# An expert layer on one core: results read back from the last put with pairs, and gathers that skip unused list places

## The reference

```python
h2 = _rmsnorm(x, ffn_norm_w).reshape(Bx * Tx, Dx)
glogits = h2 @ gate_w + gate_b
topv, topi = jax.lax.top_k(glogits, TOPK)      # TOPK = 4 of E = 32
gw = jax.nn.softmax(topv, axis=-1)
combine = jnp.zeros((N, E), x.dtype).at[jnp.arange(N)[:, None], topi].add(gw)
def body(acc, we):
    wu, wd, ce = we
    ug = h2 @ wu
    u, g = (ug[:, :DFF], ug[:, DFF:])
    return (acc + ce[:, None] * (jax.nn.silu(g) * u @ wd), None)
y2, _ = jax.lax.scan(body, jnp.zeros_like(h2), (W_up, W_down, combine.T))
return x + y2.reshape(Bx, Tx, Dx)
```

## Time and profile before

| | |
|---|---|
| median of 3 runs | 1138.51 us (1137.43 to 1142.05) |
| the profiled execution | 1133.5 us |
| its span, first to last instruction | 1131.7 us |
| busy PE, DVE, POOL, ACT | 87%, 73%, 62%, 40% of the span |
| granted TensorE clock, mean | 0.918 |
| DMA | 239.22 MB, mean 211 GB/s |
| software queue (POOL's transfers) | 40.02 MB in 19552 packets |
| expert loop, first transpose to first final sum | 676.6 to 1098.4 us |

### The profile page before, as it was taken

How to read it: one execution, slowest core, us unless ns; L and a number is a source line. 1 busy time by engine, 2 the same in 40 slices (tenths; PEclk the granted TensorE clock), 3 DMA queues, 4 the chain that set the end, 5 groups by cost and what they waited for, 6 DMA issues and landing times.

```text
span 1131.7 us, 19754 instructions
## 1 busy us (share of the span) xinstructions
PE 984.0 (87%) x6270; PEld 795.6 (70%) x6270; DVE 829.8 (73%) x1750; ACT 456.6 (40%) x1120; POOL 700.9 (62%) x654
## 2 busy tenths in 40 slices
PE   3879699998999989989987419999999999999995
PEld 2557477676776776757766308888888888888884
DVE  3878589778787788877957526777777677777778
ACT  1123243342432423333344205555555555555541
POOL 1404435757747667576585856777777777777750
PEclk8779799889898898988999659999999999999997
DMA  6237976566566555574665467776776767766599
GB/s 188 69 87 237 326 255 187 157 198 179 176 181 207 161 167 190 179 217 136 186 204 194 154 231 261 266 257 246 255 245 212 250 228 250 257 212 209 133 336 372
DMA packets 110748, 239.22 MB, mean 211 GB/s; under 512 B 19170, under 2 KB 48247, under 8 KB 109914
## 3 DMA queue, kind: packets, MB, share of 16 engines
q1 hardware_dynamic: 84042, 192.03, 51.8%
q0 software_dynamic: 19552, 40.02, 11.1%
q10 hardware_dynamic: 7056, 5.91, 1.6%
HBM read 140.37 MB, written 90.05 MB: 204 GB/s over the span
## 4 chain that ended last, share of the span: by engine, by line
PE 38%; DVE 22%; POOL 18%; issue 14%; DMA 6%; ACT 1%; SPq 0%; DVEq 0%; POOLq 0%; ACTq 0%
POOL rows_in L685 7%; PE gbank L985 7%; PE gbank L852 6%; DVE ring L1354 6%; POOL pick_rows L692 4%; POOL lists L647 4%; PE scores L813 4%; DMA rows_in<-x_rows,token_row 4%; PE gbank L1005 3%; PE gbank L777 3%; PE gbank L748 2%; POOL ring L654 1%; DVE stat L1368 1%; PE gbank L767 1%; DVE prob L1390 1%
## 5 line engine op out<-in xcount | busy, mean ns | idle before, releaser
L985 PE MATMUL gbank<-ring,in_part 128*128 x954 | 262.8, 411 | 0.1
L654 POOL TENSOR_TENSOR ring<-ring 128x512 fp32r<-128x512 f32 x96 | 121.5, 1281 | 141.7 <-ACT ring L1151 141.1
L692 POOL DMA_INDIRECT pick_rows<-rows_out,pair_row x156 | 161.6, 1036 | 56.5 <-issue 46.9
L985 PEld LDWEIGHTS gbank<-ring,in_part 128*128 128x128 f32 x954 | 168.6, 190 | 28.7 <-issue 0.3
L685 POOL DMA_INDIRECT rows_in<-x_rows,token_row x156 | 151.7, 972 | 54.2 <-issue 34.3
L647 POOL DMA_INDIRECT lists<-entry,slot_i x128 | 136.1, 1063 | 36.7 <-issue 34.1
L1005 PE MATMUL gbank<-ring,mid_part 128*128 x954 | 151.3, 294 | 0.4 <-DVE mid_part L1609 0.4
L1588 DVE SCALAR_TENSOR_TENSOR in_part<-scores,norm_w,in_part 128x128 fp32r<-128x128 f32 x318 | 96.8, 346 | 53.2 <-ACT in_part L1196 53.1
L1597 DVE SCALAR_TENSOR_TENSOR mid<-gbank,norms,silu 128x256 f32<-128x256 f32 x156 | 75.5, 484 | 74.4 <-ACT silu L1204 73.0
L852 PE MATMUL gbank<-w_o,ring 128*128 128x256 f32 x512 | 126.3, 403 | 0.6 <-ACT ring L1121 0.6
L777 PE MATMUL gbank<-h_t,w_qk 128*128 128x512 f32 x480 | 122.1, 405 | 4.7 <-DVE ring L1354 2.5
(11 more groups left out here) (171 smaller groups left out, 1553.1 us busy)
## 6 DMA issues: line engine op xcount, KB each, us to landing
w_parts<-ring SPq DMA_DIRECT2D x192, 256.0 KB, 3.2
ring<-w_parts SPq DMA_DIRECT2D x32, 1536.0 KB
ring<-in_W_up SPq DMA_DIRECT2D x64, 256.0 KB, 4.1
q_r<-rot SPq DMA_DIRECT2D x32, 512.0 KB, 6.1
picks<-pick_rows SPq DMA_DIRECT2D x8, 2048.0 KB, 22.2
lists<-in_fill_slots SPq DMA_DIRECT2D x36, 256.0 KB, 5.2
ring<-in_W_down SPq DMA_DIRECT2D x32, 256.0 KB, 3.9
x_t<-in_x_t SPq DMA_DIRECT2D x8, 512.0 KB, 4.9
```

The source lines that it names most:

```text
L654: e.tensor_tensor(lower, lower.bitcast(F32), upper.bitcast(F32), ALU.subtract).then_inc(s_lower, 1)
L692: e.indirect_dma_start(out=pick_rows, out_offset=bass.IndirectOffsetOnAxis(ap=begun_row[:, i:i + 1] if i < AHEAD else pair_row[:, i:i + 1] ...
L985: ins = e.matmul(bank[:, :], in_parts[i % 2][x][:, c, :], ring[:, bass.ds(at + y * WE + c * 2 * DFF, 2 * DFF)], start=k == 0, stop=k == le ...
```

## The change

It has four parts:

- SP waits for `s_put` itself. DVE writes four counts to `all_out`, for each of the four semaphores 16 times the number of puts with pairs on it; SP loads four numbers instead of one. ACT's wait for the last four puts and its increment go.
- Unused list places hold the token number 4096, and gathers have a bounds check at 4095, so that their rows are not fetched.
- As a left-out row keeps what the buffer held, DVE zeroes the six `rows_in` once. The buffers lie where the first part's tiles were, so DVE waits for the last entries to land before it, and POOL's gathers wait for `s_cleared`.
- The limit of `token_row` to 4095 goes.

```diff
--- before.py
+++ after.py
@@ -358,7 +358,7 @@
     plan_slot = sb("plan_slot", [1, 2 * P], I32)
     plan_wait = sb("plan_wait", [1, 2 * P], I32)
     ring_wait = sb("ring_wait", [1, E], I32)
-    all_out = sb("all_out", [1, 1], I32)
+    all_out = sb("all_out", [1, NY], I32)
     rows_in = [sb(f"rows_in{i}", [P, D]) for i in range(NG)]
     in_parts = [[sb(f"in_part{i}{h}", [P, KC, P], F32R) for h in range(2)] for i in range(2)]
     silu = [sb(f"silu{i}", [P, DFF]) for i in range(2)]
@@ -412,8 +412,8 @@
              "c_in", "d_mul", "d_sum", "u_mul", "u_add", "x0", "scaled", "w_split", "consts_b", "diag", "normed", "h",
              "q_mul", "v_s", "shift", "norm", "x2", "glog", "gsub", "picked", "filled",
              "slot_i"))
-    (s_list_tile, s_expert, s_gates, s_token_row, s_ring_wait, s_plan, s_in_lower, s_mid, s_mid_parts, s_final) = (
-        sem(f"s_{n}") for n in ("list_tile", "expert", "gates", "token_row", "ring_wait", "plan", "in_lower", "mid",
+    (s_list_tile, s_cleared, s_expert, s_gates, s_token_row, s_ring_wait, s_plan, s_in_lower, s_mid, s_mid_parts, s_final) = (
+        sem(f"s_{n}") for n in ("list_tile", "cleared", "expert", "gates", "token_row", "ring_wait", "plan", "in_lower", "mid",
                                 "mid_parts", "final"))
     s_sum, s_summed = sem("s_sum"), sem("s_summed")
     s_begun, s_begun_row = sem("s_begun"), sem("s_begun_row")
@@ -581,10 +581,10 @@
             say_ready(n)
 
 
-
         w.wait_ge(s_resid, NT // NX)
-        rows = e.value_load(all_out[0:1, 0:1], min_val=NY + 1, max_val=NET + NY)
-        e.wait_ge(s_rows_out, rows)
+        landed = [e.value_load(all_out[0:1, r:r + 1], min_val=16, max_val=16 * -(-NET // NY)) for r in range(NY)]
+        for r in range(NY):
+            e.wait_ge(s_put[r], landed[r])
         for c in range(PARTS):
             if c >= NPICK:
                 w.wait_ge(s_final, c - NPICK + 1)
@@ -685,7 +685,8 @@
             e.indirect_dma_start(
                 out=rows_in[i % NG][:, :], out_offset=None, in_=x2_rows,
                 in_offset=bass.IndirectOffsetOnAxis(
-                    ap=begun[:, i, 3:4].bitcast(I32) if i < AHEAD else token_row[:, i:i + 1], axis=0)).then_inc(s_rows_in[i % NG], 16)
+                    ap=begun[:, i, 3:4].bitcast(I32) if i < AHEAD else token_row[:, i:i + 1], axis=0),
+                bounds_check=NTOK - 1, oob_is_err=False).then_inc(s_rows_in[i % NG], 16)
 
         def scatter(i):
             w.wait_ge(s_rows_out, i + 1)
@@ -698,6 +699,7 @@
         for k in range(2 * TPM):
             w.wait_ge(s_x2_row[(LAST - k) % (2 * TPM)], 16 * ((LAST - k) // (2 * TPM) + 1))
         w.wait_ge(s_begun, 16)
+        w.wait_ge(s_cleared, 1)
         for i in range(AHEAD):
             gather(i)
         w.wait_ge(s_token_row, 1)
@@ -1229,10 +1231,6 @@
                 turn_in(i + 2)
             if i % XSTEP == 0 and 2 <= i // XSTEP < 2 + NT // NX:
                 load_x_rows(i // XSTEP - 2)
-
-        for k in range(NY):
-            w.wait_ge(s_put[(NET - 1 - k) % NY], 16 * ((NET - 1 - k) // NY + 1))
-        e.sem_inc(s_rows_out, NY)
         for c in range(PARTS):
             t = c * NP + NP - 1
             w.wait_ge(s_sum, c + 1)
@@ -1547,6 +1545,12 @@
         w.wait_ge(s_vector, got)
         e.tensor_scalar(list_tile[:, :], of_tile[:, 2, :], 1.0, float(E * LT), ALU.add,
                         ALU.min).then_inc(s_list_tile, 1)
+
+        for r in range(GROUPS - NPAY, GROUPS):
+            w.wait_ge(s_entry[r % NPAY], entries_of(r))
+        for i in range(NG):
+            ins = e.memset(rows_in[i][:, :], 0.0)
+        ins.then_inc(s_cleared, 1)
         w.wait_ge(s_vector, of_expert)
         e.tensor_scalar(of_tile[:, 3, :], of_tile[:, 0, :], float(E - 1), None, ALU.min).then_inc(s_expert, 1)
 
@@ -1569,15 +1573,20 @@
             w.wait_ge(s_turned, 6)
             got = own.mark(e.tensor_copy(pair_row[:, :], turned_rows[0]))
             w.wait_ge(s_vector, got)
-            got = own.mark(e.tensor_scalar(token_row[:, :], pair_row[:, :], 2, None, ALU.arith_shift_right))
-            w.wait_ge(s_vector, got)
-            e.tensor_scalar(token_row[:, :], token_row[:, :], NTOK - 1, None, ALU.min).then_inc(s_token_row, 1)
+
+            e.tensor_scalar(token_row[:, :], pair_row[:, :], 2, None, ALU.arith_shift_right).then_inc(s_token_row, 1)
 
         def slots():
             w.wait_ge(s_turned, 6)
             e.tensor_copy(gates[:, :], turned_rows[1]).then_inc(s_gates, 1)
             e.tensor_copy(norms[:, :], turned_rows[2]).then_inc(s_gates, 1)
-            e.tensor_scalar(all_out[:, :], ends[0:1, E - 1:E], float(AHEAD + NY), None, ALU.add)
+
+            for r in range(NY):
+                got = own.mark(e.tensor_scalar(all_out[:, r:r + 1], ends[0:1, E - 1:E], float(AHEAD + NY - 1 - r), None, ALU.add))
+            w.wait_ge(s_vector, got)
+            got = own.mark(e.tensor_scalar(all_out[:, :], all_out[:, :], 2, None, ALU.arith_shift_right))
+            w.wait_ge(s_vector, got)
+            e.tensor_scalar(all_out[:, :], all_out[:, :], 16.0, None, ALU.mult)
             e.tensor_scalar(ring_wait[:, :], ends[0:1, :], float(AHEAD + 1), None, ALU.add).then_inc(s_ring_wait, 1)
 
         def turn_in(i):
@@ -1676,7 +1685,7 @@
     scale = f(DH ** -0.5)
 
     unused = np.zeros((P, LINE), f)
-    unused[:, 0], unused[:, 3] = PAIRS + p, np.full(P, NTOK - 1, np.int32).view(f)
+    unused[:, 0], unused[:, 3] = PAIRS + p, np.full(P, NTOK, np.int32).view(f)
     mask_rows = np.zeros((P, P), f)
     mask_rows[0:T] = np.tile(np.eye(T, dtype=f), (1, 2))
     mask_rows[T:T + SINK_ROWS] = np.tile(np.repeat(np.eye(2, dtype=f), T, axis=1), (3, 1))
```

## The result

The changed kernel took 1141.62 us (median of 14 runs, 1136.24 to 1144.87), the kernel before beside it 1136.99 (14 runs, 1134.31 to 1142.05): ratio **1.0032, 95% interval [1.0017, 1.0047]**. Three later comparisons of the same two kernels gave 1.0040 [1.0017, 1.0064], 1.0085 [1.0059, 1.0112] and 1.0047 [1.003, 1.0065]. All 43 runs of the changed kernel have the mean 1142.0, the 86 runs of the kernel before beside them 1136.3: +5.7 us. The forecast was 1145.4 us and +6.9. The direction was right; the size was too large against the first comparison (0.0032 x 1137 = +3.6 us). The profiled execution took 1142.65 us, its span is 1140.8.

The account below looks back on a forecast made before the run. POOL's gather and put per tile were taken to bound the loop, with DVE's fixed sums behind. 7.55 + 0.2 - 0.8 = +6.9 us on the median of 1138.5 gave 1145.4 us, range 1136.5 to 1149.5.

Parts of the forecast that it names:

- What bounds the kernel: Expert loop: POOL's gather and put, 2.60 us a tile, set the pace, PE close behind at 2.53; DVE's sums follow.
- one sign of being wrong: Expert loop and tail: forecast wrong if POOL's unbroken row gets pauses or the tail is no longer DVE's alone.
- The check on the gathers, +7.55: POOL's loop: the bounds check adds 50 ns to each of 151 gathers in an unbroken row, +7.55 us.
- Rival B: POOL's gathers: the check is free or disappears in the 0.30 us gap; 1137.9 us, chance 0.17.
- C: POOL's gathers: left-out rows make descriptor generation cheaper, -4.1 us on POOL; 1133.6 us in all, chance 0.09.
- The left-out rows, -0.8: End of the loop: the last gathers, now empty, land in 6.7 instead of 7.54 us, -0.8; ends 0 and -2.9.
- Start, +0.2: Loop's head: one DVE operation less for token_row, a MOVE, and slots()'s extra operations and waits, +0.2 us (0 to 0.8).
- Zeroing and plan, 0: Before the loop: DVE's six memsets take 1.6 us, the plan ends 3.9 us before the first transpose; cost 0.
- Rival D: Start: the plan's registers load too late, PE starts 3 us later or more; 1148.4 us and above, chance 0.12.
- its sign, a first transpose after 677: PE's start: first transpose expected still at 676.6 us; one after 677 would mean the plan's registers came too late.
- Reading back and ACT, 0: After the loop: earlier reading back and ACT's dropped wait are worth 0, as DVE's sums wait for no pick.
- a bound of 5.7: Whole kernel: about 0.5%, 5.7 us, tells from no change; above 1144.2 us is slower, below 1132.8 faster.

Follow-up runs that it names:

- f1: The kernel before with the bounds check on its gathers and nothing else, at the usual speed: ratio 1.0057 [1.0034, 1.0079].
- f3: The kernel before with only the change's reading back (SP waits for the puts, ACT for none behind its loop): ratio 0.9997 [0.997, 1.0024].
- h3: The changed kernel with the old wait ahead of the reading back and ACT's old wait for the last four puts: ratio 1.0076 [1.0046, 1.0107] to the kernel before.
- f4: The kernel before with six result buffers instead of four, so reading back starts two results later: ratio 1.0023 [0.9993, 1.0052].
- g4: The kernel before with unchecked puts (unused places get rows of their own) and six result buffers: ratio 1.0008 [0.9982, 1.0034].
- g1: The kernel before with unchecked puts, unused places naming rows of their own (3968 more rows written): ratio 0.9973 [0.9949, 0.9997].
- g3: The kernel before with unchecked puts (unused places get rows of their own) and the change's earlier reading back: ratio 0.9957 [0.9931, 0.9982].
- g2: The kernel before with a one-element memset on POOL between each gather and its put: ratio 1.0001 [0.9976, 1.0026].
- e1: The kernel before with the bounds check on its gathers and nothing else, in the group where the kernel before took 1243.56 us: ratio 1.0023 [0.9993, 1.0053].

## Why the prediction was wrong in size

**What bounds the kernel: right.** POOL's row set the pace, PE's waits for rows rose by 7.6 us (forecast about 7), and the unchecked puts moved the time the other way. But one sign of being wrong that the prediction had named did come: the row got pauses, one at its head in all seven kernels with the check.

**The check on the gathers, +7.55: right in kind, a little small.** It is 55 ns an instruction, not 50. The loops of the seven kernels with the check are 403.2 to 406.5 us long (mean 405.1), those of the five with it on the puts alone 394.0 to 397.2 (mean 395.7): +9.4 in 150 steps. The 149 steps behind the first make **+8.1** of it, as 149 x 0.055 = 8.2 says; the rest is the start. Rival B is dead, and so is C: empty gathers took the median 1022 like full ones (the minimum in the row is 1015), and the left-out rows shortened no descriptor generation.

**The left-out rows, -0.8: too small.** The landing fell from 8.1 us (mean of the five kernels with the check on the puts alone) to 6.2 (mean of the five profiles with rows left out), **-1.9**; within the range of 0 to -2.9 that was given. The 6.7 of an empty put under load was too near to the 7.54 of one profile, whose landing was the shortest of its kind. The Trainium skill, page "DMA: Bandwidth & Descriptors", section "Why a DMA increments its semaphore by 16 and not by 1", has all 16 engines post their +1 whatever the shape of the transfer. The profiles don't show these posts; they show that an empty gather still took over 6 us to land and that the packets stayed 19552. What the prediction made of it, that an empty gather queues as long as a full one, did not come out: the landing was 1.9 us shorter.

**Start, +0.2: too small, +1.2.** The first gather of the row starts 13.5 us after the first transpose in both profiles (676.6 to 690.1, 677.7 to 691.2), but the step behind it took 4.0 us on average with the check and 2.8 without. The prediction had said that gathers 0 to 7 pay nothing, as POOL is idle ahead of its first put, and that PE leads at the head. POOL had the time, PE did not: the gathers from tile 3 on started 0.2 to 0.5 us later after the first transpose (3.9 to 4.1 instead of 3.6), the next one had 0.05 more to issue and landed later, and PE waited for it. Why it landed as late as 6.3 to 7.0 us after its start, where an unchecked one was used after 5.8, is open. f1, the check alone, has this pause too; so it comes from the check and not from the zeroing or the left-out rows.

**Zeroing and plan, 0: right.** 1.64 us of memsets against 1.6 estimated; the plan ended 3.8 us ahead of the first transpose (3.9 estimated). Rival D is dead, although its sign, a first transpose after 677, was met (677.7): over all profiles this transpose scatters from 674.1 to 686.9, so the sign was too sharp.

**Reading back and ACT, 0: right.** f3 and h3 show it from both sides, f4, g4 and g1 where it would end: DVE's sums waited 2.0 to 3.8 us at leads of 25.3, 25.7 and 30.0 us, and above that only 0.3 in g3.

**The sum.** With the measured sizes it is 8.1 + 1.2 - 1.9 = +7.5 by the profiles (the loop's 9.4 less 1.9), near the +6.9 forecast; that they are near is in part luck, as the start's excess and the landing's cancel. The times say +5.7 over all runs (1.0 either way, twice the standard error from the spread of 2.6 us among runs), +3.6 in the first comparison. What takes the other 2 us is **not settled**. The four profiled executions of the changed kernel have the mean 1143.8, 1.8 above all its runs, and a mean over five and seven loops that scatter by 1.2 us is itself uncertain by more than 1 us, so it may be nothing but scatter. Groups also differ among each other by more than their intervals say (1.0032 to 1.0085 for one pair of kernels), and the last three ran on different chips. The left-out rows and the reading back were tried as its cause and showed nothing in the times.

**The step that failed** is the last one, in which the sum was worked out on one execution and set in full on the median of three runs, as if both stood in the middle of their kind. Neither did. The median, 1138.5, lies 1.5 us above the 1137.0 that the same kernel took in the first comparison, whose fourteen runs begin with these three; the profiled execution, 1133.5, lies 3.5 below that 1137.0, and that of the changed kernel, 1142.65, lies 1.0 above its own median. Of the miss of 3.8 us (1145.4 against 1141.6) the base makes 1.5. The other 2.3 are the difference itself, forecast as 6.9 and measured as 4.6 by the medians of this comparison, 3.6 by its ratio. The terms don't explain them: measured, the check (+8.1 for +7.55) and the start (+1.2 for +0.2) cost more than forecast, and only the landing (-1.9 for -0.8) less. Why less than their sum reached the times stays open. And with a sum of +6.9 beside a bound of 5.7, 0.52 for slower against 0.42 for the same was as much as could be said; over all runs the change costs 0.50%, which is that bound.

## What to carry to other kernels

Where GpSimd issues indirect DMAs without a pause, their instructions of about 1 us set the pace; the option that saved 4 MB but lengthened each instruction by 55 ns was a loss here. Giving unused places harmless rows of their own, so that neither side has a check, and reading back earlier was 0.43 and 0.46% faster in two groups. A transfer started earlier was worth nothing while its lead was 31 us and DVE waited for no part; measure that lead before and after a change of pace, since a faster loop can use it up. At the head of a loop look at each engine's own slack: POOL's 2.6 us of idle time there did not help PE, which waited for the gather of tile 4. And a term of under 1% should be judged against several profiles and all runs of both kernels, not against one execution.

## What the runs showed of the hardware that was not expected

- The bounds check on an indirect gather costs 55 ns (967 to 1022) and on an indirect put 32 (1017 to 985). The Trainium skill, page "DMA: Bandwidth & Descriptors", section "Anatomy of one DMA — SWDGE (gpsimd) path", calls descriptor generation small; here the instructions in which POOL does it, about 1 us each, are the bound of a loop of 400 us.
- A gather whose 128 rows are all out of bounds takes as long to issue as a full one (1015 to 1024 ns), and its landing is 1.9 us shorter (6.2 against 8.1).
- Behind an indirect DMA on POOL there are 0.30 us in which a memset of 0.09 us ran for free (g2, 1.0001).
- The gather of tile 4, the second from `token_row`, was used 5.8 us after its start without a wait in eight of the nine kernels with unchecked gathers, and landed only after 6.3 to 7.0 us in the seven with checked ones.
- In one of five groups every kernel took 9% longer, nearly all of it in the expert loop (499 us instead of 403 in the same kernel on the same chip, e1 and f1), and there the check cost nothing that the intervals show.
